# Eighteen tiles' second norm moved between partitions by DMA and turned in blocks by VectorE

## What is computed

```python
x = x + xattn(layernorm(x), ctx, ctx, W_proj, b_proj)     # 16 heads of 32, keys within 64 rows of the query
x = x + ffn(layernorm(x), ...)                            # x: 8 batches x 512 rows x 512

def ffn(x, ...):                                          # a scan over the 8 batches
    def step(c, xt):
        ft = sigmoid(xt @ wf.T + c @ uf.T + bf)
        it = sigmoid(xt @ wi.T + c @ ui.T + bi)
        gt = tanh(xt @ wc.T + c @ uc.T + bc)
        return ft * c + it * gt, None
    c_final, _ = lax.scan(step, c0, x)
    return tanh(einsum('tbi,oi->tbo', x, wo) + c_final @ uo.T + bo)
```

## Time and profile before

| what | value |
|---|---|
| time, median of 3 runs | 956.67 us (954.79 to 958.66) |
| the profiled execution's own time | 956.46 us |
| its span from first to last instruction | 954.6 us |
| mean granted TensorE clock | 0.997 of 2.4 GHz |
| TensorE matmul busy | 924.4 us (97%), 7888 matmuls |
| VectorE busy | 664.2 us (70%) |
| ScalarE busy | 476.3 us (50%) |
| GpSimd busy | 202.9 us (21%) |
| DMA packets | 99604, 9384 of them under 512 bytes |

### The profile page before, as it was taken

How to read it: one execution, slowest core, us unless ns; L and a number is a source line. 1 busy time by engine, 2 the same in 40 slices (tenths; PEclk the granted TensorE clock), 3 DMA queues, 4 the chain that set the end, 5 groups by cost and what they waited for, 6 DMA issues and landing times.

```text
span 954.6 us, 21946 instructions
## 1 busy us (share of the span) xinstructions
PE 924.4 (97%) x7888; PEld 723.1 (76%) x7888; DVE 664.2 (70%) x2263; ACT 476.3 (50%) x1430; POOL 202.9 (21%) x228
## 2 busy tenths in 40 slices
PE   5889999899999999999999999999999999999998
PEld 3545666688888888888888888888888888878887
DVE  6888898878779877897789867986798522142222
ACT  5887667655445544655545546555555412131222
POOL 4475322211111111111111111111111000003444
PEclk9999999999999999999999999999999999999999
DMA  9554422233333334333433234333322040049862
GB/s 287 166 163 149 117 88 75 67 104 93 95 107 116 108 104 111 106 107 106 115 109 100 83 104 117 95 85 84 96 85 68 24 154 1 1 161 389 294 246 100
DMA packets 99604, 114.15 MB, mean 120 GB/s; under 512 B 9384, under 2 KB 66728, under 8 KB 97960
## 3 DMA queue, kind: packets, MB, share of 16 engines
q1 hardware_dynamic: 98776, 112.47, 37.8%
q10 hardware_dynamic: 720, 0.27, 0.2%
HBM read 82.98 MB, written 29.74 MB: 118 GB/s over the span
## 4 chain that ended last, share of the span: by engine, by line
PE 88%; DVE 4%; ACT 3%; issue 3%; POOL 1%; DMA 1%; SPq 0%; DVEq 0%; ACTq 0%; POOLq 0%
PE ps_g L633 18%; PE ps_g L635 17%; PE ps_g L634 17%; PE ps_a L670 5%; PE ps_a L692 5%; PE ps_m L633 4%; PE ps_v L713 3%; PE ps_m L635 3%; PE ps_m L634 3%; PE ps_m L745 2%; PE ps_v L718 2%; ACT probs L841 2%; PE ps_a L633 2%; PE ps_a L635 2%; PE ps_a L634 2%
## 5 line engine op out<-in xcount | busy, mean ns | idle before, releaser
L841 ACT ACTIVATE probs<-probs,rowmin 128x192 f32<-128x192 f32 (+1 forms) x512 | 239.5, 470 | 87.7 <-DVE rowmin L948 87.6
L948 DVE CUSTOM_DVE_ANT_0 probs<-ps_a,mask 128x192 f32<-128x192 f32 (+1 forms) x512 | 167.3, 386 | 50.5 <-PE ps_a L670 49.7
L883 ACT ACTIVATE gate<-ps_g,bias 128x512 f32<-128x512 f32 x84 | 57.7, 687 | 183.5 <-PE ps_g L635 183.1
L633 PE MATMUL ps_g<-state_hi,gate_w 128*128 128x512 f32 x336 | 133.5, 397 | 0.0
L635 PE MATMUL ps_g<-state_hi,gate_w 128*128 128x512 f32 x336 | 131.1, 390 | 0.0
L634 PE MATMUL ps_g<-state_lo,gate_w 128*128 128x512 f32 x336 | 130.8, 389 | 0.0
L983 DVE STREAM_TRANSPOSE keys<-probs 32x128 f32<-32x128 f32 x420 | 126.0, 300 | 5.4 <-issue 0.2
L841 ACT ACTIVATION_READ_ACCUMULATOR probs<-probs,rowmin 128x1 f32 x512 | 96.4, 188 | 0.0
L612 POOL TENSOR_TENSOR attn_lo<-recip,attn_hi 128x512 fp32r<-128x512 f32 x23 | 29.8, 1294 | 283.4 <-ACT attn_hi L854 283.4
L846 ACT ACTIVATE probs_t<-ps_a 128x512 f32<-128x512 f32 x108 | 59.4, 595 | 51.9 <-PE ps_a L692 51.9
L633 PE MATMUL ps_g<-x2t_even,gate_w 128*128 128x512 f32 x192 | 80.0, 417 | 0.0
(11 more groups left out here) (203 smaller groups left out, 1723.2 us busy)
## 6 DMA issues: line engine op xcount, KB each, us to landing
values<-ctx_rows SPq DMA_DIRECT2D x34, 256.0 KB, 4.4
xr<-x SPq DMA_DIRECT2D x32, 256.0 KB, 3.9
keys<-ctx_t SPq DMA_DIRECT2D x16, 512.0 KB, 4.9
x_dram<-xr SPq DMA_DIRECT2D x32, 256.0 KB, 5.4
gate_w<-x2t_dram SPq DMA_DIRECT2D x8, 1024.0 KB, 10.0
keys<-ctx_t SPq DMA_DIRECT2D x16, 384.0 KB, 3.5
x2t_dram<-x2t_even SPq DMA_DIRECT2D x12, 512.0 KB, 3.9
x2t_dram<-x2t_odd SPq DMA_DIRECT2D x12, 512.0 KB, 3.9
```

Of the source, the lines that this page charges most:

```text
L633: pe.matmul(ps, lhs[0], rhs[0], start=start, stop=False)
L841: act.activation(row, row, ACT.Exp, bias=rowmin[:, i % 2, h:h + 1], scale=-1.0, accum_out=rowsum[:, i // G % 2, i % G, h:h + 1]).then_inc( ...
L883: act.activation(gate[:, min(gt, 1), :], ps_g[i % 2][:, :], ACT.Tanh, bias=(first_bias if b == 0 else bias)[:, gt, m:m + 1], scale=1.0 if ...
L948: dve.tensor_tensor_reduce(probs[:, i % 2, h, 0:SEEN[t]], ps_a[h][:, score_at[i]:score_at[i] + SEEN[t]], mask[:, MASK0[t]:MASK0[t] + SEEN[ ...
```

## The change

For the tiles in `MOVED` (8, 9, 10, 12, 13, 14 and so on to 30: eighteen tiles, all from tile 8 on but the last of each batch) TensorE's four transposes are gone. Instead, right after "ln2b", SP issues sixteen DMAs. Each one takes 32 partitions of `tile_row` and, of each 128 columns, one run of 32 (128 bytes), and writes them to another group of 32 partitions of the part of `x2t` that will hold the low half. That puts every 32x32 block at the place where it belongs after a transpose. At the end of the second round VectorE turns all blocks with one instruction of 128x512 from there back into `tile_row`, ScalarE rounds from `tile_row` into the high half, and VectorE subtracts into the low half. The steps "turn2" and "turn2_lo" of these tiles move to behind the second round's last seven cells; SP's "norm_rows" now waits for the low half, since the broadcast rows overwrite `tile_row`. Waits that counted TensorE's transposes count only the tiles that are still turned there.

```diff
+    MOVED = [j for j in range(SENT - 1, TILES) if j % TT < TT - 1]
...
-            if s == 2:
+            if s == 2 and i - 1 not in MOVED:
                 tile_steps("turn2", i - 1)
             gates(2)
             steps.extend(("score", m) for m in ahead[:1])
-            if s == 2:
+            if s == 2 and i - 1 not in MOVED:
                 tile_steps("turn2_lo", i - 1)
...
             else:
+                if i - 1 in MOVED:
+                    tile_steps("turn2", i - 1)
+                    tile_steps("turn2_lo", i - 1)
                 if i + 2 < TILES:
                     steps.append(("norm_rows", i))
...
                     sp.dma_start(x1_rows[i], xr[:, i % XR, :]).then_inc(x1_out[i % XR], DMA)
+                    if i in MOVED:
+                        sp.wait_ge(x2_done, i + 1)
+                        if t == 0:
+                            sp.wait_ge(gate_sum, UNITS * (b - 1))
+                            sp.wait_ge(x2t_out[b % 2], DMA * TT * (b // 2))
+                        for a in range(0, P, BLK):
+                            blocks = x2[a:a + BLK, :].rearrange("p (k m c) -> p k m c", m=P // BLK, c=BLK)
+                            for m in range(P // BLK):
+                                home = x2t[b % 2][BLK * m:BLK * (m + 1), 1, :, t * P + a:t * P + a + BLK]
+                                sp.dma_start(home.bitcast(F32), blocks[:, :, m, :]).then_inc(x2_moved, DMA)
...
-                    sp.wait_ge(x2_turned, i)
+                    sp.wait_ge(x2_turned, by_tensor(i))
+                    if i - 1 in MOVED:
+                        sp.wait_ge(x2_lo, i)
...
-                if kind == "turn2":
+                if kind == "turn2" and i not in MOVED:
                     pe.wait_ge(x2_done, i + 1)
...
+                    if i in MOVED:
+                        act.wait_ge(x2_blocks, moved(i + 1))
+                        act.activation(x2t[b % 2][:, 0, :, t * P:(t + 1) * P], x2[:, :].rearrange("p (k q) -> p k q", k=G),
+                                       ACT.Copy).then_inc(x2_hi, 1)
+                        continue
...
+                if kind == "turn2" and i in MOVED:
+                    b, t = i // TT, i % TT
+                    dve.wait_ge(x2_moved, moves_landed(i + 1))
+                    dve.transpose(x2[:, :].rearrange("p (k q) -> p k q", k=G),
+                                  x2t[b % 2][:, 1, :, t * P:(t + 1) * P].bitcast(F32)).then_inc(x2_blocks, 1)
...
                     dve.wait_ge(x2_hi, i + 1)
+                    if i in MOVED:
+                        dve.tensor_tensor(x2t[b % 2][:, 1, :, cols], x2[:, :].rearrange("p (k q) -> p k q", k=G),
+                                          x2t[b % 2][:, 0, :, cols].bitcast(F32), ALU.subtract).then_inc(x2_lo, 1)
+                        continue
```

## The result

| | before | after |
|---|---|---|
| time, median of the runs taken side by side (four of each) | 956.42 us | 1014.08 us (1011.8 to 1017.14) |
| ratio, 95% interval | | 1.0608 (1.0576 to 1.0639) |
| span of the profiled execution | 954.6 us | 1014.0 us |
| mean granted TensorE clock | 0.997 | 0.975 |
| DMA packets under 512 bytes | 9384 | 50856 |

The kernel became 6.1% slower, 58 us. The forecast was 969 us with a range up to 985, so the time lies beyond its far end.

The account below looks back on a forecast made before the run. TensorE, busy nine tenths or more from about 190 us, was taken as the bound. Six times (2.75 lost in first tiles, less 0.25 and 0.44 gained in second and third) made 12.4 us: 956.5 + 12.4 = 968.9 us, range 953 to 985.

Parts of the forecast that it names:

- the mechanism in the first tiles: First tile of a batch: VectorE waits for the landing, so the second value product starts 2.75 us later.
- The chain: Block turn, ScalarE's rounding and subtraction in series, with three handovers, ahead of the second slot's side turns: 2.1 us.
- The blend's halves: On VectorE, the first half, held up by GpSimd's bias addition, falls from 1.67 to 0.69 us: 1.0 us gained.
- The transposes: Four fewer on TensorE per moved tile give 0.44 us each, 7.9 us for eighteen tiles.
- The rival of quick issues: SP issues at 0.32 us land before VectorE arrives in all kinds: +0.7 us, 957.2 us; chance 0.26.
- The landing time: Sixteen SP issues at 0.58 us, the last landing 1.95 us after its start: 418.5 in the first kind.
- The slack: Between VectorE's side turns and the second value product: 0.24 us in first tiles, 1.9 us in second and third.
- the sign of being wrong: TensorE waiting in all eighteen rounds would mean that the landing takes longer than the small transfer's row says.
- slower still: Rival: SP's issues held up, at 0.7 us each all kinds wait another 1.8 us, over 985 us; chance 0.07.
- What is queued behind: Work behind SP's moves and low half, and ScalarE's rounding: covered, nothing, or some 0.3 us inside the 2.75.
- The clock: Rival: TensorE's idle time in first tiles brings half clock, 1.7 us lost six times, 10.2 us, 979.1 us; chance 0.20.
- chances for the three outcomes: For the whole kernel against a 0.5% threshold, about 4.8 us: slower 0.63, same 0.26, faster 0.11.

Follow-up runs that it names:

- `next_tile_load_first`: Changed kernel with landed blocks used one round later and SP's load of a later tile's rows between the first and last eight moves: 950.21 us, ratio 0.9948.
- `half_the_moves`: Changed kernel with eight of the sixteen DMAs per moved tile issued and waited for, half of each tile not carried over: 955.56 us, ratio 0.9998.
- `round_behind_copies`: Changed kernel with ScalarE's rounding of a moved tile put behind its copies of turned probabilities in the next round: 1021.37 us, ratio 1.0683.
- `no_moves`: Changed kernel without SP's sixteen issues, the block turn reading a constant tensor, order on all engines kept: 956.07 us, ratio 0.9997.
- `loads_first`: Changed kernel with SP's store of the halves and broadcast rows of a moved tile put behind the next tile's loads: 1004.65 us, ratio 1.0516.
- `third_tiles_only`: Changed kernel with only the third tile of each batch moved, six tiles: 961.25 us, ratio 1.0049.
- `filled`: Changed kernel with ten matmuls of unused result put on TensorE ahead of the scores at eleven places where it stood: 1004.78 us, ratio 1.0524.
- `half_by_gpsimd`: Changed kernel with all sixteen moves made, eight issued by SP and eight by GpSimd: 960.18 us, ratio 1.0033.

## Why the prediction was wrong

**What held.** The direction, and the mechanism in the first tiles. The chain is 0.71 + 0.70 + 0.69 = 2.10 us, as put. From the block turn's start to the value product tile 16 takes 5.37 us and tile 17 takes 4.42 us, where the forecast's terms make 5.4 and 4.4. The blend's halves take 0.68 and 0.69 us in all eighteen tiles, so the 1.67 us of the earlier trace rows came back. (What the prediction cites there from the Trainium skill is said of a GpSimd operation that reads SBUF; the bias addition reads `xr` and `bp_row`, so the condition is met.) The transposes are worth about 6 us by two runs, give or take one, somewhat less than the 7.9 put: with half the moves a gain of that size and 6.1 us of waits cancel, and `next_tile_load_first` has 5.0 us of gain with 1.0 us of waits left. The rival of quick issues (957.2) is what `half_the_moves` shows (955.6). That VectorE's work leaves TensorE so little slack was read rightly.

**The landing time was undersized.** The step was sixteen issues at 0.58 us, the last landing 1.95 us after its start: 10.75 us. The issues of the changed kernel (ns min/median/max, first and last start, and the time to landing):

```profile
L527 SPq DMA_DIRECT2D x2t_even<-tile_row x144: 595/601/1704, 203.2 to 714.5; - x144
...
DMA to landing us min/median/max: 1.8/1.9/3.2
```

The timeline line of tile 16 above has sixteen issues in 10.79 us. The next issue starts 0.64 us after the one before in the median, 0.04 us after its end; and in fifteen of the eighteen rows of sixteen one issue takes much longer, 0.93 to 1.70 us. That makes a mean distance of 0.69 us (0.68 for tile 16), and 15 x 0.69 + 1.85 = 12.2. The measured landings are 11.6 to 12.9 us after the normed tile in sixteen tiles, 13.8 in tile 8 and 14.2 in tile 30. The duration of a usual issue was right to 4%; it was taken for the distance from start to start, and the long issue in a row was left out of the sum. The earlier trace rows has durations of up to 1.59 us, which the forecast used for a rival alone. For TensorE's transposes I had minded the difference between duration and distance.

Put into the forecast's own sum, a landing 1.35 us later gives 4.1 us for a first tile, 1.1 for a second and 0.4 for a third, about 33 us for six of each, and a time of 990 us. So this term accounts for about 21 of the 45 us by which the forecast was short. The other 24 us are the clock and what one tile's wait does to the next, below.

**The slack was used up.** The forecast let the second and third tiles gain 0.25 and 0.44 us: their landing at 10.75 us comes 1.4 and 0.5 us after VectorE's arrival and puts the side turns off by 1.6 and 1.0 us, within the slack of 1.9. With 0.9 to 2.1 us more (tiles 8 and 30 above that) all eighteen wait, which is the sign of being wrong that the prediction itself names. TensorE's idle times are 2.0 to 4.2 us in the first tiles (19.4 in six), 0.7 to 1.9 in the second (8.1) and 1.2 to 3.6 in the third (15.0). The rival named "slower still" had this, with issues held up and 0.7 us for each, at over 985 us. It got 0.07, though the distance that it needed was nearly the one that the kernel had.

**"What is queued behind" was nearly nothing in the sum and was not.** Two things stood there. On ScalarE the copies behind the rounding were given 0.3 us and the value product as the one that waits; in fact the scores wait for them, 29.2 us in sixteen rounds. It cost little by itself, as `round_behind_copies` shows. On SP the next tile's loads behind the low half were called covered in the second and third kinds. They were not: 13.6 us of waits for the queries, against 5.3 us before, and the normed tile of tile 18 comes 2.6 us nearer to VectorE's need (7.67 us, by the earlier trace rows 465.65 - 455.39 = 10.26 before). The sum of such waits is no price by itself: `no_moves` has 11.5 us of the same wait and loses nothing, since no moves stand behind it. `loads_first` and `third_tiles_only` show the carrying over, some 9 us of it.

**The clock was a rival and is a part.** It had a chance of 0.20 and six times 1.7 us. There are nine stretches of low clock, of 3.4 or 6.8 us, since long idle times came in the first and third tiles and five stretches are twice as long as the one of the earlier trace rows. Their worth is 8 to 11 us as `filled` measured it, up to 16 as estimated there, 23 us at most. So the 10.2 us of the rival were about the right size, in part by luck, since they came from six stretches of half the length; and its being an alternative was not right. An idle time that is longer than the one seen, in a forecast that has six of them, should have been in the forecast itself.

**What stays open.** How the last 19 us part between the second tiles and what they carry over, how much of the 24 us is clock, and why `round_behind_copies` is 0.7% slower than the changed kernel; its trace has 48.6 us of TensorE's idle time where that has 42.6. Why one issue in a row is long is not shown either. (The prediction's chances for the three outcomes are off by a hundredth: its parts make 0.64 for slower and 0.10 for faster.)

## What to carry to other kernels

A row of transfers from one queue has landed after the number of issues times the mean distance from start to start, plus one landing. That mean distance, with the long issues in it, is what to read in the trace, and not the usual duration of an issue; compare it with the slack for every kind of place, since eight issues cost nothing here and sixteen 6%. Where a landing is late, use the data a stage later or share the issues between two queues before giving up the change: both took away more than nine tenths of the loss, the first one with a gain over the kernel before. When a wait is put into a full engine's path, price its clock with it, and follow the waiting engine's queue, and SP's, to the next tile.

## What the runs showed of the hardware

- An SP issue from SBUF to SBUF with 128 pieces of 128 bytes takes 0.60 us in the median, and the next one starts 0.64 us after it. In fifteen of eighteen rows of sixteen such issues one took 0.93 to 1.70 us. In the median it lands 1.9 us after it is issued.
- On GpSimd such issues take 0.55 us each, but every row of eight had one pause inside, of 2.9 to 5.2 us (tile 17's 2.94 us after seven issues, tile 16's 4.38 us after one). The pauses stand before every seventh issue, counted through the whole trace of `half_by_gpsimd`: after 7, 6, 5, 4, 3, 2 and 1 issues of a row, then after 7 again.
- VectorE's turn of 32x32 blocks over 128x512 float32 takes 0.71 us (711 ns), where 212 ns for 32 columns and 300 ns for 128 had given an estimate of 0.65 us.
- In the changed kernel each single idle time of TensorE from 2.26 us up between 200 and 850 us (eight, up to 3.38 us) came with 3.4 or 6.8 us at a granted clock of 0.5; of the shorter ones only one of 1.82 us did. That is no fixed border: in `round_behind_copies` one of 2.72 us (ended at 277.66) and in `loads_first` one of 2.35 us (ended at 382.83) were passed at full clock, and in `half_by_gpsimd` one of five idle times of 1.1 to 1.4 us (ended at 528.02) came with 3.4 us of low clock.
